# Routed feed-forward steps: bias tables held on chip as three bfloat16 parts, and spare weights copied on chip

## The reference, cut to what matters

```python
def _fff(x, nw, nb, w1, b1, w2, b2, act):
    node = zeros
    for _ in range(8):                       # walk the tree
        logit = einsum('bsd,bsd->bs', x, nw[node]) + nb[node]
        node = 2 * node + 1 + (logit > 0)
    leaf = node - 255
    h = act(einsum('bsd,bsdl->bsl', x, w1[leaf]) + b1[leaf])
    return einsum('bsl,bsld->bsd', h, w2[leaf]) + b2[leaf]
# xn: the 2048 normalised tokens
q, k, v = (_fff(xn, *net, relu) for net in ("q", "k", "v"))
att = softmax(q @ k.T / sqrt(128));  y = xn + att @ v
return y + _fff(y, *f, gelu)
```

## Time and profile before

| | us |
|---|---|
| median of 3 runs | 2674.63 (2674.29 to 2676.77) |
| span of the profiled execution | 2667.1 |
| median less that span | 7.5 |
| attention of layer 0 and the preparation of the routes | to about 372 |
| steps of q, k and v | about 372 to 584 |
| small attention and the route of f | about 584 to 673 |
| steps of f, last gather | about 673 to 772 |
| layer 1 (not touched) | about 780 to the end |

### The profile page before, as it was taken

One profiled execution on the slowest core, in us unless ns is written; L12 is line 12 of the kernel. 1 busy time (PEld: TensorE's weight loads), 2 busy tenths in 40 slices (PEclk: granted clock), 3 DMA queues, 4 the chain that ended last, 5 costly groups with the idle time before them and its releaser, 6 DMA issues.

```text
span 2667.1 us, 92816 instructions
## 1 busy us (share of the span) xinstructions
PE 2337.9 (88%) x35088; PEld 1640.0 (61%) x35116; DVE 1935.3 (73%) x3019; ACT 1764.5 (66%) x3676; POOL 1511.0 (57%) x1116
## 2 busy tenths in 40 slices
PE   7999669874847777779999999999999999999995
PEld 5666346653533344346777777777777777777774
DVE  5888452223218888778888888888888888888883
ACT  5777413332326677557888778887778887878883
POOL 3666142232024444556777777777777777777770
PEclk9999779997868899889999999999999999999997
DMA  9100037840520000011121122111121211121111
GB/s 335 53 0 0 21 92 211 236 139 20 137 88 1 0 0 0 0 33 33 31 55 48 32 47 63 40 31 52 44 54 31 55 48 31 41 69 40 31 31 33
DMA packets 143485, 153.91 MB, mean 58 GB/s; under 512 B 12272, under 2 KB 111920, under 8 KB 142256
## 3 DMA queue, kind: packets, MB, share of 16 engines
q1 hardware_dynamic: 139312, 144.53, 19.8%
q0 software_dynamic: 4096, 8.40, 1.1%
HBM read 75.29 MB, written 27.26 MB: 38 GB/s over the span
## 4 chain that ended last, share of the span: by engine, by line
PE 50%; DVE 3%; issue 2%; PEld 1%; DVEq 1%; ACT 0%; PEldq 0%; POOL 0%; POOLq 0%; ACTq 0%
PE ps L2050 12%; PE ps L2145 6%; PE ps L2061 6%; PE ps L2093 5%; PE ps L2114 5%; PE ps L2171 4%; PE ps L2082 4%; PE ps L2104 3%; PE ps L2180 3%; PE ps L2074 1%; PE ps L2160 1%; PE ps L2153 1%; DVE a L2544 1%; DVE ss L2552 1%; DVE bq L2545 1%
## 5 line engine op out<-in xcount | busy, mean ns | idle before, releaser
L2448 POOL TENSOR_TENSOR c<-a,bq 128x1024 f32<-128x1024 f32 x192 | 454.0, 2365 | 241.6 <-DVE bq L2545 241.1
L2458 POOL TENSOR_TENSOR qn<-c,ss 128x1024 f32<-128x1024 f32 x192 | 376.7, 1962 | 28.4 <-issue 4.3
L2050 PE MATMUL ps<-wqk,xs 128*128 128x512 f32 x768 | 371.9, 607 | 11.7 <-POOL xs L2441 9.7
L2544 DVE TENSOR_TENSOR a<-ps,tab 128x512 f32<-128x512 f32 x384 | 262.9, 685 | 15.9 <-ACT sq L2255 5.9
L2545 DVE TENSOR_TENSOR bq<-ps,tab 128x512 f32<-128x512 f32 x384 | 261.5, 681 | 0.0
L2466 POOL TENSOR_TENSOR z<-z,sm 128x1024 f32<-128x1024 f32 x96 | 182.7, 1903 | 129.2 <-DVE sm L2573 129.2
L1511 POOL TENSOR_TENSOR hC<-hs,Cs 128x1024 f32<-128x1024 f32 x64 | 150.2, 2353 | 175.7 <-ACT Cs L1663 88.5
L2552 DVE TENSOR_REDUCE ss<-sq 128x16 f32<-128x1024 f32 x192 | 229.3, 1215 | 27.3 <-issue 16.6
L2255 ACT ACTIVATE sq<-ps 128x512 f32<-128x512 f32 x384 | 215.4, 596 | 27.6 <-PE ps L2050 25.3
L2050 PEld LDWEIGHTS ps<-wqk,xs 128*128 128x128 f32 x768 | 140.3, 193 | 137.2 <-issue 130.9
L2061 PEld LDWEIGHTS ps<-ident,qn 128*128 128x128 f32 x1536 | 176.5, 141 | 67.5 <-issue 47.4
(11 more groups left out here) (319 smaller groups left out, 5260.4 us busy)
## 6 DMA issues: line engine op xcount, KB each, us to landing
Vw<-Vs SPq DMA_DIRECT2D x192, 256.0 KB, 4.1
win_rows<-rows_q SPq DMA_DIRECT2D x24, 256.0 KB, 3.1
outs_q<-win_out SPq DMA_DIRECT2D x24, 256.0 KB, 3.3
wqk<-in_wqkv SPq DMA_DIRECT2D x6, 1024.0 KB, 5.0
leaves<-in_f_w SPq DMA_DIRECT2D x9, 576.0 KB, 4.5
leaves<-in_q_w SPq DMA_DIRECT2D x1, 4608.0 KB, 18.8
leaves<-in_k_w SPq DMA_DIRECT2D x1, 4608.0 KB, 22.6
leaves<-in_v_w SPq DMA_DIRECT2D x8, 576.0 KB, 4.5
```

The lines of the kernel that those rows point to most:

```text
L2050: nc.tensor.matmul(jobs.out(n), xs[:, t * 128:(t + 1) * 128], wqk[:, (2 * y + s) * 512:(2 * y + s + 1) * 512], start=True, stop=True).then ...
L2448: nc.gpsimd.tensor_tensor(f(c), f(a), f(bq), ALU.add).then_inc(c_ready.sem, 1)
L2458: nc.gpsimd.tensor_tensor(qn[:, t, y, :, :, :].rearrange("p h s e -> p h (s e)"), c[:, y, :, :, :].rearrange("p h s e -> p h (s e)"), spre ...
L2544: nc.vector.tensor_tensor(a[:, y, :, s, :], Zs, spread(table(0, s), H1), ALU.mult)
```

## The change

The bias tables of all four nets are loaded once as float32 (`tabs`, 1 MB) into the buffer that will later be `leaves_1`. In the first iteration of `attention0` DVE splits them into three bfloat16 parts that add up to the float32 value (`split_piece`, four pieces), SP moves the parts on chip into `leaf_parts` with 12 transfers, one part above the other on 96 partitions, and only then loads `leaves_1`. The leaf masks are made for 96 rows, as bfloat16, so that one bfloat16 matmul over 96 rows adds a bias. The array is no longer divided in `H` and `O`, and each of them has one bank and one eviction in place of two halves; the banks alternate from step to step. The drains and extra semaphores after evictions go; the engines wait for the bank's own count (`taken`).

A spare window's weights are no longer fetched. In DVE's steps with `g` < 8, after its two evictions, `stage` copies two windows' weights and tables from the resident set: two register loads and three copies each. Renewals no longer carry tables, wait until all spares of the net are copied, and are issued 11 steps after the own step, one a step.

```diff
@@ attention0, VectorE, the first iteration only
+                        if s >= 4 and not not_first(it):
+                            core.routed.split_piece(nc, dve, s - 4)
@@ class Routed
-RENEW = ((7, 4), (8, 5), (9, 6), (10, 7), (11, 0), (13, 1), (15, 2), (17, 3))
+RENEW = tuple((WG - 1 + g, g) for g in range(8))
+    def split_piece(self, nc, dve, i):
+        c = slice(512 * i, 512 * i + 512)
+        rest, (high, mid, low) = self.whole[:, c], (self.parts[:, q, c] for q in range(NPART))
+        dve.wait_ge(self.whole_in, 16)
+        nc.vector.tensor_copy(high, rest)
+        dve.drain()
+        nc.vector.tensor_tensor(rest, rest, high, ALU.subtract)
+        dve.drain()
+        nc.vector.tensor_copy(mid, rest)
+        dve.drain()
+        nc.vector.tensor_tensor(low, rest, mid, ALU.subtract).then_inc(self.split, 1)
     def load(self, core, sp):
+        sp.dma_start(self.whole, core.dram["tabs"]).then_inc(self.whole_in, 16)
...
+        sp.wait_ge(self.split, 4)
+        for n in range(4):
+            for q in range(NPART):
+                sp.dma_start(self.tabs[32 * q:32 * q + 32, n, :, :]..., self.parts[32 * n:32 * n + 32, q, :])
+        sp.wait_ge(self.moved, 16 * 4 * NPART)
+        self.load_set(core, sp, 1, self.loads)
@@ routed0, SyncE
-                def spare(n, i):
...
                 def renew(n, g):
-                    sp.wait_ge(*filled(f"O{(n - 2) * WG + (g if 4 <= g else 8 + g)}.1"))
+                    sp.wait_ge(staged, 4 * (n - 1))
+                    sp.wait_ge(*filled(f"O{(n - 2) * WG + g}"))
@@ routed0, TensorE
-                        nc.tensor.matmul(out(f"OH{s}"), agree_b[:, :], node[:, s % 2, :], start=True, stop=True)
+                        nc.tensor.matmul(out(f"OH{s}")[0:NROW, :], agree_b[:, :], node[:, s % 2, :], start=True, stop=True)
...
-                        for j in range(2):
-                            q = slice(64 * j, 64 * j + 64)
-                            nc.tensor.matmul(out(f"H{s}.{j}")[:, 0:T], tab[q, at, 0:128], oh[q, s % 3, j * T:(j + 1) * T],
-                                             start=True, stop=False, tile_position=(64 * j, 0))
+                        if g < 8:
+                            nc.tensor.matmul(out(f"H{s}"), table_of(n, g, 0)[:, 0:128], oh[:, s % 3, :], ...)
+                        else:
+                            for w in range(4):
+                                nc.tensor.matmul(out(f"H{s}")[:, tile(w)], table_of(n, g, w)[:, 0:128], oh[:, s % 3, tile(w)], ...)
...
-                        for pair in ((0, 2), (1, 3)):
+                        for w in range(4):
+                            nc.tensor.matmul(out(f"O{s}")[:, tile(w)], oh[:, s % 3, tile(w)], table_of(n, g, w)[:, 128:256], ...)
+                        for w in range(4):
+                            last = nc.tensor.matmul(out(f"O{s}")[:, tile(w)], hid[:, s % 2, tile(w)], last_of(n, g, w), ...)
@@ routed0, VectorE
+                def stage(n, w):
+                    if w == 0:
+                        if n >= 2:
+                            dve.wait_ge(R.again[R.set_of(n)], 16 * 8)
...
+                    if w % 4 == 0 and n > 0:
+                        dve.wait_ge(*filled(f"O{n * WG - 4 + w // 4}"))
+                    chunk = dve.value_load(chunk_of[0:1, n, w:w + 1], ...)
+                    group = dve.value_load(group_of[0:1, n, w:w + 1], ...)
+                    own = R.w[R.set_of(n)][:, bass.ds(chunk, 1), :].rearrange("p c k -> p (c k)")
+                    nc.vector.tensor_copy(front[w], own[:, 0:160])
+                    nc.vector.tensor_copy(last_w[n][:, w, :], own[:, 160:WROW])
+                    done = nc.vector.tensor_copy(spare_tab[:, w, :], R.tabs[:, n, bass.ds(group, 1), :]...)
...
+                    s = t - 1
+                    if lo <= s < hi and s % WG < 8:
+                        for w in (2 * (s % WG), 2 * (s % WG) + 1):
+                            stage(net_of(s), w)
```

More of the change, by code:

```diff
@@ L654, in __init__ @@
         self.w = [sb(f"leaves_{i}", [128, NCHUNK, WROW]) for i in range(2)]
-        self.tab = [sb(f"leaftab_{i}", [128, NCHUNK // 4, 2 * 128]) for i in range(2)]
+        self.tabs = sb("leaf_parts", [NROW, 4, NCHUNK // 4, 2 * 128], BF16)
+        wide = self.w[1][:, :, :].rearrange("p c k -> p (c k)")
+        self.whole = wide[:, 0:2048]
+        self.parts = wide[:, 2048:2048 + NPART * 1024].bitcast(BF16).rearrange("p (q m) -> p q m", q=NPART)
         self.zero = sb("zero_row", [128, D])
@@ L914, in step @@
                         pe.wait_ge(*free(f"N{s}"))
                         for w in range(4):
[L916 removed]
+                            last = nc.tensor.matmul(out(f"N{s}")[32 * w:32 * w + 32, tile(w)], first_of(n, g, w)[:, 128:160],
                                                     xw[:, s % 4, tile(w)], start=True, stop=True, tile_position=(0, 32 * w))
                         last.then_inc(sem_filled(f"N{s}"), 1)
[L919 to L920 removed]
+                    for s, n, g in stage(2):
+                        pe.wait_ge(*taken(f"N{s}"))
@@ new lines, in step @@
+                    for s, n, g in stage(3):
+                        pe.wait_ge(*taken(f"OH{s}"))
+                        pe.wait_ge(*free(f"H{s}"))
+                        if g < 8:
+                            nc.tensor.matmul(out(f"H{s}"), table_of(n, g, 0)[:, 0:128], oh[:, s % 3, :],
+                                             start=True, stop=False, skip_group_check=True)
+                        else:
+                            for w in range(4):
+                                nc.tensor.matmul(out(f"H{s}")[:, tile(w)], table_of(n, g, w)[:, 0:128], oh[:, s % 3, tile(w)],
+                                                 start=(w == 0), stop=False, skip_group_check=True)
+                        for w in range(4):
+                            last = nc.tensor.matmul(out(f"H{s}")[:, tile(w)], first_of(n, g, w)[:, 0:128], xw[:, s % 4, tile(w)],
+                                                    start=False, stop=(w == 3), skip_group_check=True)
+                        last.then_inc(sem_filled(f"H{s}"), 1)
@@ new lines, in step @@
+                    for s, n, g in stage(4):
+                        pe.wait_ge(*taken(f"H{s}"))
+                        pe.wait_ge(*free(f"O{s}"))
+                        for w in range(4):
+                            nc.tensor.matmul(out(f"O{s}")[:, tile(w)], oh[:, s % 3, tile(w)], table_of(n, g, w)[:, 128:256],
+                                             start=(w == 0), stop=False, skip_group_check=True)
+                        for w in range(4):
+                            last = nc.tensor.matmul(out(f"O{s}")[:, tile(w)], hid[:, s % 2, tile(w)], last_of(n, g, w),
+                                                    start=False, stop=(w == 3), skip_group_check=True)
+                        last.then_inc(sem_filled(f"O{s}"), 1)
```

163 lines of the change are left out of this document (66 added, 97 removed).

## The result

The changed kernel takes 2582.86 us (median of 4 runs, 2580.92 to 2586.95) against 2674.46 beside it (4 runs, 2673.54 to 2676.77): a ratio of 0.9666 with a 95% interval of 0.965 to 0.9681, 91.6 us less. The forecast was 2601, with 2580 to 2640, so the time lies 2.9 us inside the range's lower end.

What follows compares the result with a forecast made beforehand. TensorE was taken to set the routed steps at 4.96 us, GpSimd's gathers to bound next. Terms -55.1 (gather v), -23.7 (f) and +5 (split) make -73.8 us: span 2593.3, plus 7.5 around it, 2601 us, range 2580 to 2640.

Steps and rivals of the forecast that it cites:

- The step of TensorE: Routed steps: X, N and OH 1.21 us, eight float32 products 1.72, biases 0.5; taken as 3.5 us, ends 3.3 and 4.0.
- GpSimd is late next: Ahead of the small attention: GpSimd's paired gathers of 48.6 us set gather v at 532.7 instead of 587.81, 55.1 us gained.
- The rival "quicker": First attention and gathers: the split is hidden and gathers land sooner without spare transfers, 2585 us; chance 0.04.
- gather q starts straight behind scatter v: GpSimd's chain: free of scatter v at 435.5, after net q's results at 431.4, so gather q starts at 435.5, not 455.76.
- VectorE's loads: Staging steps: register loads and address work, 1.72 us a step, overlap VectorE's computing; about 3.2 us, hidden behind TensorE's 3.5.
- as the rival had it: Staging steps: loads in series, so VectorE sets these steps at 4.6 us; 2618 us, chance 0.24.
- wrong if full own steps exceed 4.0: Sign in the routed steps: the forecast of 3.5 us a step is wrong if full own steps exceed 4.0 us.
- f: The f net, with no gather beside it: 57.4 us today, 34.9 after; with 1.2 off step 4, 23.7 us gained.
- The split: First attention's first iteration: four pieces of 2.5 us, 4.2 hidden in idle slots; 5 us lost, ends 0 and 10.
- The rule weighed: GpSimd's issues beside VectorE's copies in the steps: 0.08 us more each, 1 us in all, left out.
- The sum: Whole kernel: -55.1 - 23.7 + 5 = -73.8 us, span 2593.3; with 7.5 us around the span, 2601 us.

Runs made afterwards that it cites:

- experiment 3: Kernel after, with chunk and group of the staging copies taken from constants instead of registers loaded from memory: 2581.4 us, ratio 0.9653 to the kernel before.
- Experiment 9: Kernel after, with the bias products of H and O float32 again over the undivided array: 2636.41 us, ratio 0.987 to the kernel before.
- experiment 2: Kernel after, without the waits after each pair in the gathers of q and k: 2574.9 us, ratio 0.9634 to the kernel before.
- experiment 10: Kernel after, plus two unused 147 KB weight transfers to DRAM after each put of a net's first eight steps: 2590.08 us, ratio 0.971 to the kernel before.
- experiment 4: Kernel after, with the split's four VectorE pieces ahead of the rotary products of their slot instead of behind: 2582.62 us, ratio 0.9656 to the kernel before.

## Why the prediction was right or wrong

- *The step of TensorE*: 3.5 forecast, 3.43 measured, and by its terms: 1.21 and 1.14, 1.72 and 1.84, 0.5 and 0.45. Without the register loads the steps are 3.42 us apart (experiment 3). Experiment 9 shows the cause, the type of the biases.
- *GpSimd is late next*: right, and shown by taking the pauses away (experiment 2). Forecast of gather v, with its own 5 us for the split, 537.7; measured 533.02. Two misses lie in it and nearly cancel. The split put everything 5.5 us later than forecast. And the chain was quicker: from scatter q to gather q it took 93.5 us instead of 94.8, the first gather 47.2 and the second 41.1 instead of 48.6 each. I priced every pair at the mean wait of before (3.94 us), though the last pairs run when the steps' transfers are over. The rival "quicker" named this; putting traffic back (experiment 10) brought 4.4 of the second gather's 7.5 us. That gather q starts straight behind scatter v did not hold in this trace: it waited for the last put of net q.
- *VectorE's loads*: the step of the prediction that failed in mechanism. I took them as hidden, with a step of 4.6 us as the other end. They are half hidden: the first pair runs beside the evictions, the second in series. A load takes 0.31 us on VectorE, the address work behind it 0.19, where I had 0.27 and 0.105 from SyncE's rows:

```profile
L1295 DVEq TENSOR_LOAD <-spare_chunk x64: 296/306/724, 389.3 to 649.2; - x64
L1295 DVEq FUSED_REGOPS  x64: 190/190/207, 389.9 to 649.5; - x64
```

  (columns: minimum, median and maximum in ns, first and last start). So VectorE sets the staging steps, as the rival had it, at 3.75 us on average (threshold to threshold, 120.0 us for all 32) and not at 4.6. It cost little: in the four spare steps behind each eight VectorE catches up, so that the twelve steps of q and of k took 41.6 and 42.6 us, about 3.5 each, and GpSimd covers the rest up to gather v. In f nothing covers it: 5.2 us there (experiment 3). The sign "wrong if full own steps exceed 4.0" was met by four of the 32, of 4.07 to 4.72 us; in f by 643.74 - 639.62 = 4.12.
- *f*: from the first threshold to gather f 677.02 to 750.76 before, 621.47 to 671.83 after, 23.4 us less; forecast 23.7. Two misses cancel: the eight staging steps took 651.28 - 621.47 = 29.8 us, 1.8 more than at 3.5, and the three steps between the thresholds of the spare ones 659.35 - 651.28 = 8.1, 2.4 less: VectorE, by then 2.4 us behind TensorE's products, catches up as soon as it stages nothing, and the first two of these thresholds lie 1.37 us apart.
- *The split*: 5 forecast, 10.0 measured at by_norm and after, the upper end of its bounds. The 4.2 us of idle time did hide as much as forecast: 4 pieces took 3.4 + 3.7 + 3.9 + 3.8 = 14.8 us, less 4.2 is 10.6. The mis-sized term is the piece, 3.7 us instead of 2.5, by the lock.
- *The rule weighed*: I asked whether GpSimd's issues would lose a VectorE copy, and left it out on the earlier trace rows. The forecast that issues lose little was right, with 0.94 to 0.99 us for those beside copies. It was the copies that lost:

```profile
451.20 0.94 POOL L1149 DMA_INDIRECT work_b<-outs_q,slot  x1 [4.26 <-DMA work_b<-outs_q,slot]
451.75 0.44 DVE L1299 COPY work_c<-leaves 128x128 f32 x1
```

  None of the 121 staging copies away from issues took over 0.25 us. Of the 71 beside one, 19 took 0.27 to 0.46, most of them ending about when the issue did; that is some 2 us in all. And the same rule struck where I had not looked, at the pieces beside GpSimd's sums. The Trainium skill, "SBUF — State Buffer", section "SBUF: two separate sides", says that the pair of ports is "an **exclusive lock**, not a bandwidth split", held for a whole instruction, and that VectorE needs it in its two-port modes, which copies and casts can enter, and for two SBUF inputs against a GpSimd operation that reads SBUF. The trace agrees to 0.02 us, for casts and for subtractions (experiment 4), and VectorE's products with a PSUM operand were free at 0.68 us.
- *The sum*: forecast -73.8, and -78.9 measured at the start of layer 1, by the terms above. The other 13 us that separate 2601 from 2583 were in no term: layer 1 is 9.0 us shorter, and what lies around a span is 2.3 us, not 7.5: the trace of before was of an execution some 5 us under the median. One trace could not tell these apart. That the sum of the terms came within 5.1 us is in part luck, since misses cancel in gather v and in f.

## What to carry to other kernels

When the bound moves to a chain of waits for landings (here GpSimd's pairs), time won ahead of it can be lost in it again, as in experiment 3, where faster steps load the queues that the chain lands through; ask first whether the chain needs its waits. A float32 product that carries only selected constants cost a quarter here as bfloat16 parts stacked along the rows (0.22 us against 0.86). Price added VectorE work that stays within SBUF with what GpSimd runs beside it, and a wait at its value in the traffic of its moment, not at its mean.

## What the runs showed of the hardware

- VectorE's cast or subtraction within SBUF waits for the end of a GpSimd tensor operation beside it: 0.43 us became up to 1.46, 0.69 up to 1.60. GpSimd's sum of 1.27 us became up to 1.50 where VectorE's cast had begun first.
- VectorE's copies of 0.21 to 0.24 us within SBUF took up to 0.46 beside GpSimd's issue of an indirect transfer; the issue stayed at 0.94 to 0.99 in the kernel after.
- Two register loads with their address work (2 x (0.31 + 0.19) us) between copies left VectorE idle for 1.0 to 1.8 us; moved ahead of all copies, the loads of a step left it idle for 1.0 to 2.1.
- In layer 1 single images take 31.4 us instead of 30.55, before and after the change: eight in the two traces of before, four in three of the twelve after. The cause is open.
